# Two attention layers in fp32: groups 2 and 3 of layer 1 split as well, sums seeded by plain DMAs, and four smaller shifts in order

## The chip, the cores and the metric

The kernel runs on one core of one Trainium2 chip. The metric is the device time of one execution in microseconds. Before the change three runs took 3254.99, 3256.44 and 3256.32 us, median 3256.32. A change within about 0.2% is not told from none.

## What is computed

The input x is 4 x 128 x 64 x 64 in fp32: four images b of C = 128 channels and N = 4096 positions. Two attention layers follow each other.

```
layer 0 (inner width 64):
  g, theta, phi = g_w x + g_b, theta_w x + theta_b, phi_w x + phi_b
  y = softmax(theta^T phi) g          # over 4096 keys
  x1 = W_w y + W_b + x
layer 1 (width 128):
  q, k, v = Wq x1 + bq, (sum over o of Wk) * x1 + bk, Wv x1 + bv
  out = x1 + softmax(q^T k / sqrt(128)) v
```

The phi and k biases and the q bias are scaled by 64, so the scores are large, and the softmax needs an exact maximum shift and products of nearly full fp32 precision.

## The kernel before

**Stages and blocks.** A stage is one layer of one image, and there are eight: layer 0 of images 0 and 1, then layer 1 of 0, layer 0 of 2, layer 1 of 1, layer 0 of 3, layer 1 of 2, layer 1 of 3 (`run_all`). A stage has 8 blocks of 512 queries, numbered g over the whole program, 64 in all. A block walks over the 4096 keys in 16 groups `s`; a group is two key tiles of 128, and its scores are 128 keys x 1024 (two tiles x 512 queries) in PSUM, double buffered as `scores[:, s % 2]`. While one stage runs, its blocks also prepare the keys and values of a later one: phi and g (`prepares="phi"`), k and v (`"kv"`), or k and v with v held aside in `hold` and `g_vals` (`"late"`, the stage before the last). The last stage prepares nothing.

**Each engine has its own written order.** `block_program` of an engine goes through s = 0 to 15 and issues what falls due at that group; constants such as `G_AT`, `MOVES_AT`, `PIECES_AT` say at which. Engines meet only at semaphores. An instruction that waits holds all that comes behind it on its engine.

**Rough pieces.** The softmax shift is the row maximum of rough scores. For the next block's 512 queries, 32 matmuls (`rough_piece`, L510), four query tiles by eight key chunks, go into two PSUM banks of `rough` in turn, and DVE reduces each (`reduce_piece`, L924). `PIECES_AT` gives two pieces to most groups and three to four of them (in layer 1 s = 7, 8, 10, 12). In layer 1 a group with three issues one piece ahead of its scores and two behind. DVE then builds a diagonal (L931), PE turns it into a row (`shift_row`, L516) at s = 15.

**Layer 0.** Scores of a tile are two fp32r matmuls (L534, L537). ACT takes the exponential straight from PSUM (L841). POOL adds the 16 groups up in `sums` (L385, `add`). The values are full fp32 matmuls, two column halves at a time (L573, `value_batch`).

**Layer 1.** Scores of a tile are three fp32r matmuls (L539, L540, L543), high by high, high key low part by query, key by low query part. DVE adds the shift row from PSUM into one of six SBUF buffers `probs` (L941). ACT takes the exponential twice: rounded to fp32r into one of four `p_hi` buffers (L834), and in place (L835, semaphore `s_whole`). POOL subtracts the two into `p_lo` (`split_probs`, L1046, `s_p_lo`). PE multiplies three groups behind the scores (`LAG` = 3): per tile `p_hi v_hi`, `p_lo v_hi`, `p_hi v_lo` (`halved_values`, L559 to L561). So the value matmuls of group 13, 14 and 15 run at s = 0, 1, 2 of the next block. Groups 2 and 3, `WHOLE`, are the exception: no `p_hi`, no split, but true fp32 matmuls with `v_vals` (`value_group`, L582), each recorded as two instructions, so four a group.

**The sums of layer 1.** For the denominators the 16 exponentials are summed in two tiles `sent_sums[:, 0]` and `[:, 1]`. POOL first seeds them with additions of groups 0 + 1 and 2 + 3 (`seed`, L1078), then for each of groups 4 to 15, right behind its split, POOL issues a DMA that adds the group into tile s % 2 (`send`, L1089, `accum_op=add`, 512 KB). A send waits until the one two groups before has landed. In the next block at s = 2 POOL folds both tiles into `total` (`fold`, L367, L371); PE makes denominators (L607) at s = 5.

**Low part of the queries.** ACT copies the projected queries twice, plain (`q_whole`) and rounded (`qry_a`); POOL subtracts into `qry_b` at s = 9 (`split_q`).

**Late values.** In the last block of the stage before the last, and in the first of the last, ACT moves held v chunks into `v_hi`, and POOL subtracts into `v_lo` (`split_held`), at the groups in `MOVES_AT`.

**SP's queue** in a block: load x_kv, load x_q, then wait for the previous block's result, store it, load the residual.

Of the kernel before, what the change touches and what calls it, by code (L numbers as in the profile page):

```python
# [51 lines left out]
WHOLE_CHUNK = 1  # L52
WHOLE = (2, 3)
HALVED = tuple(s for s in range(16) if s not in WHOLE)
SEEDS = 2
SEED_AT = {2: 0, 3: 2}
SENT = tuple(range(4, 16))
# [46 lines left out]
def build(nc, x, consts, out):  # L104
# [16 lines left out]
    with ExitStack() as ctx:  # L121
# [21 lines left out]
        v_vals = sb("v_vals", [P, QB])  # L143
        v_hi = sb("v_hi", [P, BLOCKS - 1, QB], F32R)
        v_lo = sb("v_lo", [P, BLOCKS - 1, QB], F32R)
# [6 lines left out]
        q_whole = sb("q_whole", [P, QB])  # L152
# [7 lines left out]
        diag = sb("diag", [P, 2, QB], F32R)  # L160
        piece_max = sb("piece_max", [P, SUB, BLOCKS])
        sums = sb("sums", [P, GC])
        sent_sums = sb("sent_sums", [P, TPG, GC])
# [4 lines left out]
        rdiag = sb("rdiag", [P, 2, QB], F32R)  # L168
        result = sb("result", [P, QB])
# [51 lines left out]
        s_seed = sem("s_seed")  # L221
        s_sent = [sem(f"s_sent_{n}") for n in range(TPG)]
# [75 lines left out]
        def seeded(nth, s):  # L298

            return nth * SEEDS + s // 2 + 1  # L300

        def sent(nth, s):

            return 16 * (nth * len(SENT) // TPG + (s - SENT[0]) // TPG + 1)

        def v_lows(b, c):

            return b * (BLOCKS - 1) + v_chunk(c) + 1

        def v_chunk(c):  # L310

            return c - (c > WHOLE_CHUNK)
# [4 lines left out]

        def summed(eng, nth, s):

            if s < 2 * SEEDS:  # L320
                eng.wait_ge(s_seed, seeded(nth, s))
            else:
                eng.wait_ge(s_sent[s % TPG], sent(nth, s))
# [15 lines left out]
        def probs_free_1(eng, st, s):  # L339

            if s >= SHARP_BUFS or st.prev == 1:
                nth, g, last = st.nth, st.g, s - SHARP_BUFS
                if last < 0:
                    nth, g, last = st.prev_nth, st.g - 1, last + GROUPS
                if last in WHOLE:
                    eng.wait_ge(s_used, used(g, last))
                else:
                    eng.wait_ge(s_p_lo, halved(nth, last))
# [10 lines left out]
        def fold(eng, layer, g, nth):  # L359
# [13 lines left out]
        def add(eng, st, s):  # L373
# [5 lines left out]
            if s == 1:  # L379
                if st.prev == 0:  # L380
                    eng.wait_ge(s_fold, st.g)
# [5 lines left out]
        def halved(nth, s):  # L387

            return nth * len(HALVED) + HALVED.index(s) + 1
# [784 lines left out]
```

## Time and profile before

| | |
|---|---|
| median of three runs | 3256.32 us |
| the profiled execution | 3254.69 us |
| its span, first to last instruction | 3252.9 us |
| PE busy | 3204.8 us (99%) |
| POOL busy | 3020.9 us (93%) |
| DVE, ACT busy | 2088.1 us (64%), 1897.1 us (58%) |
| granted TensorE clock | 0.998 |

The busy time of an engine is the union of its instructions' spans. Matmuls overlap in the records, since their ends are modelled: the distance from one start to the next is PE's pace, not the length of a record. A block is read here from one shift-row matmul (L516) to the next.

### The profile page before, as it was taken

To read this page: it belongs to the slowest core of one execution; us is meant where nothing else is said; L and a number is where in the kernel's file an instruction comes from. 1 tells how busy PE (TensorE), PEld (TensorE's weight loads), DVE (VectorE), ACT (ScalarE), POOL (GpSimd) and SP (SyncE) were. 2 spreads that over 40 slices of the span, in tenths; PEclk is the share of its full clock that TensorE was granted. 3 is DMA by queue.
4 is the path that set the end of the run, shared out by engine and by line. 5 is a ranking of instruction groups with operands and counts; after the bars stand their busy time and mean duration, and the time that the engine had idled before them with its cause. 6 is when DMAs were issued, how large, how long until landed. Compare 5 with 4: busy or idle time off the path is not lost. (4 is left out here: it accounts for less than half of the span.)

```text
span 3252.9 us, 38831 instructions
## 1 busy us (share of the span) xinstructions
PE 3204.8 (99%) x13636; PEld 2199.8 (68%) x13636; DVE 2088.1 (64%) x3036; ACT 1897.1 (58%) x2473; POOL 3020.9 (93%) x1611
## 2 busy tenths in 40 slices
PE   8999999999999999999999999999999999999997
PEld 5555555557777775555777776555577777777775
DVE  5555555556777765555777776555577777777773
ACT  5555455556666665455666665555566666666665
POOL 6988999998999999999999999999899999999998
PEclk9999999999999999999999999999999999999999
DMA  1000000004665640000565664000066675657566
GB/s 52 26 20 26 23 27 26 27 23 94 136 136 119 143 101 27 26 27 27 107 142 114 141 131 101 22 22 26 27 136 136 125 144 115 128 117 143 117 136 120
DMA packets 91922, 271.45 MB, mean 83 GB/s; under 512 B 10192, under 2 KB 10192, under 8 KB 91728
## 3 DMA queue, kind: packets, MB, share of 16 engines
q0 software_dynamic: 55296, 201.35, 32.2%
q1 hardware_dynamic: 36432, 67.62, 6.8%
q8 instruction: 108, 1.77, 0.2%
q14 instruction: 86, 0.70, 0.1%
HBM read 50.83 MB, written 16.78 MB: 21 GB/s over the span
## 5 line engine op out<-in xcount | busy, mean ns | idle before, releaser
L924 DVE TENSOR_REDUCE piece_max<-rough 128x1 f32<-128x512 f32 x2032 | 1314.7, 683 | 657.1 <-PE rough L510 646.9
L1046 POOL TENSOR_TENSOR p_lo<-probs,p_hi 128x1024 fp32r<-128x1024 f32 x448 | 1191.4, 2712 | 64.4 <-ACT probs L835 54.0
L385 POOL TENSOR_TENSOR sums<-sums,probs 128x1024 f32<-128x1024 f32 x448 | 1067.1, 2382 | 110.4 <-ACT probs L841 70.3
L941 DVE TENSOR_TENSOR probs<-scores,shift_rows 128x1024 f32<-128x1024 f32 x512 | 626.2, 1223 | 470.1 <-PE scores L543 466.9
L841 ACT ACTIVATE probs<-scores 128x1024 f32<-128x1024 f32 x512 | 521.0, 1024 | 654.3 <-PE scores L537 653.5
L834 ACT ACTIVATE p_hi<-probs 128x1024 fp32r<-128x1024 f32 x448 | 474.5, 1059 | 558.6 <-DVE probs L941 558.4
L510 PE MATMUL rough<-keys_a,qry_a 128*128 128x512 f32 x2032 | 714.2, 420 | 11.3 <-POOL keys_a L1046 3.2
L835 ACT ACTIVATE probs<-probs 128x1024 f32<-128x1024 f32 x512 | 535.7, 1046 | 88.8 <-DVE probs L941 88.8
L510 PEld LDWEIGHTS rough<-keys_a,qry_a 128*128 128x128 f32 x2032 | 366.4, 188 | 276.5 <-DVE piece_max L924 151.9
L1089 POOL DMA_DIRECT2D sent_sums<-probs x384 | 442.3, 1152 | 0.2 <-issue 0.2
L539 PE MATMUL scores<-qry_a,keys_a 128*128 128x512 f32 x1024 | 425.7, 416 | 0.0
L534 PE MATMUL scores<-qry_a,keys_a 128*128 128x512 f32 x1024 | 423.3, 413 | 0.0
L537 PE MATMUL scores<-qry_b,keys_b 128*128 128x512 f32 x1024 | 403.2, 394 | 0.0
L543 PE MATMUL scores<-qry_b,keys_a 128*128 128x512 f32 x1024 | 399.8, 390 | 0.0
L540 PE MATMUL scores<-qry_a,keys_b 128*128 128x512 f32 x1024 | 399.8, 390 | 0.0
L573 PE MATMUL acc_out<-probs,g_vals 128*64 128x512 f32 x1536 | 371.9, 605 | 0.0
L559 PE MATMUL acc_out<-p_hi,v_hi 128*128 128x512 f32 x896 | 351.9, 393 | 8.7 <-POOL p_lo L1046 8.7
L561 PE MATMUL acc_out<-p_hi,v_lo 128*128 128x512 f32 x896 | 349.2, 390 | 0.0
L560 PE MATMUL acc_out<-p_lo,v_hi 128*128 128x512 f32 x896 | 348.8, 389 | 0.0
L534 PEld LDWEIGHTS scores<-qry_a,keys_a 128*128 128x128 f32 x1024 | 192.6, 188 | 98.2 <-issue 36.5
L539 PEld LDWEIGHTS scores<-qry_a,keys_a 128*128 128x128 f32 x1024 | 192.7, 188 | 57.4 <-issue 17.3
L540 PEld LDWEIGHTS scores<-qry_a,keys_b 128*128 128x128 f32 x1024 | 192.4, 188 | 53.9 <-issue 15.1
(94 smaller groups left out, 3172.6 us busy)
## 6 DMA issues: line engine op xcount, KB each, us to landing
sent_sums<-probs POOLq DMA_DIRECT2D x384, 512.0 KB, 4.9
x_q<-x SPq DMA_DIRECT2D x32, 256.0 KB, 2.7
x_res<-x SPq DMA_DIRECT2D x32, 256.0 KB, 2.9
mid<-mid_new SPq DMA_DIRECT2D x32, 256.0 KB, 2.2
x_kv<-mid SPq DMA_DIRECT2D x32, 256.0 KB, 2.7
x_q<-mid SPq DMA_DIRECT2D x32, 256.0 KB, 2.7
x_res<-mid SPq DMA_DIRECT2D x32, 256.0 KB, 4.5
out<-result SPq DMA_DIRECT2D x32, 256.0 KB, 3.4
```

The costliest lines, as they stand in the source:

```text
L385: eng.tensor_tensor(sums[:], sums[:], probs[:, slot(st, s)], ALU.add).then_inc(s_plus, 1)
L510: mm(place, qry_a[:, parity, t * P:(t + 1) * P], cols(keys, c), start=True, stop=True).then_inc(s_rough, 1)
L534: mm(place, hi[:, k], qa, start=True, stop=False)
L539: mm(place, hi[:, k], qa, start=True, stop=False)
L540: mm(place, lo[:, k], qa, start=False, stop=False)
L834: nc.scalar.activation(hi_part(s), place, ACT.Exp, scale=SCALES[1])
L835: nc.scalar.activation(place, place, ACT.Exp, scale=SCALES[1]).then_inc(s_whole, 1)
L841: nc.scalar.activation(probs[:, slot(st, s)], scores[:, s % 2], ACT.Exp, scale=SCALES[0]).then_inc(s_whole, 1)
L924: nc.vector.reduce_max(piece_max[:, t, c:c + 1], src, AX.X).then_inc(s_reduced, 1)
L941: nc.vector.tensor_tensor(probs[:, slot(st, s)].rearrange("p (h c) -> p h c", c=QB), scores[:, s % 2].rearrange("p (h c) -> p h c", c=QB), ...
L1046: nc.gpsimd.tensor_tensor(dst, w, rd(hi), ALU.subtract).then_inc(done, 1)
L1089: nc.gpsimd.dma_start(sent_sums[:, s % TPG], probs[:, slot(st, s)], accum_op=ALU.add).then_inc(s_sent[s % TPG], 16)
```

## The change

- `WHOLE` is gone. All 16 groups of layer 1 are split: each gets `p_hi`, a split on POOL and six fp32r value matmuls. `v_vals` and `value_group` go; `v_hi` and `v_lo` have all eight chunks.
- The seeds go. SP copies groups 0 and 1 into the two sum tiles with plain DMAs (`copy_probs`), POOL sends groups 2 to 15. The sum tiles exist twice, by parity of the block. For groups 14 and 15 the send stands ahead of the split, for the others behind.
- `q_whole` goes. ACT makes `qry_a` alone, ahead of group 15's exponential in both layers (in layer 0 it stood behind). DVE makes `qry_b` from PSUM at the end of its block. The second rough piece of a block waits for that.
- In layer 1 the first of three rough pieces goes between the two score tiles of its group.
- `G_AT` for blocks that follow a layer 1 block goes from 11 to 12. The held values are moved at other groups, three in the one block and five in the next; before it was five (one without a split) and three.
- `diag` and `sums` now lie in other tiles' memory.

```diff
-PHI_AT, G_AT = (11, 9), (13, 11)
+PHI_AT, G_AT = (11, 9), (13, 12)
-MOVES_AT = ({6: 0, 8: 1, 10: 2, 12: 3, 14: 4}, {1: 5, 3: 6, 5: 7})
+MOVES_AT = ({6: 0, 9: 1, 12: 2}, {5: 3, 7: 4, 9: 5, 11: 6, 13: 7})
-Q_LO_AT = 9
-WHOLE_CHUNK = 1
-WHOLE = (2, 3)
-SEED_AT = {2: 0, 3: 2}
-SENT = tuple(range(4, 16))
+COPIED = (0, 1)
...
+        def summed(eng, nth, s):
+            if s in COPIED:
+                eng.wait_ge(s_copied[s], 16 * nth + 16)
+            else:
+                eng.wait_ge(sent_sem(nth, s), sent(nth, s))
...
+            def copy_probs(st, s):                                   # SP
+                sp.wait_ge(s_whole, whole_of(st.g, s))
+                if s == COPIED[0]:
+                    sp.wait_ge(s_fold, st.g - (st.prev == 1))
+                settle(sp)
+                sp.dma_start(sent_sums[:, st.parity, s], probs[:, slot(st, s)]).then_inc(s_copied[s], 16)
...
                 if st.next_q:
                     load_q(st.g + 2, *st.next_q)
+                if st.layer == 1:
+                    for s in COPIED:
+                        copy_probs(st, s)
...
                     place = scores[:, s % 2, h * QB:(h + 1) * QB]    # PE, score_group
+                    if h == 1 and between is not None:
+                        between()
...
+                    if m == 1:                                       # PE, piece
+                        pe.wait_ge(l_q, st.g + 2)
...
-                    if st.layer == 1 and st.nxt is not None and at[s] == 3:
-                        piece()
-                    score_group(st, s)
+                    score_group(st, s, piece if st.layer == 1 and st.nxt is not None and at[s] == 3 else None)
...
-                    if s == GROUPS - 1 and st.next_q:                # ACT
-                        take_q_whole(st.g + 2, st.next_q[0], two_banks(1))
...
+                    if s == GROUPS - 1 and st.next_q:
+                        act.wait_ge(s_scores, (st.g + 1) * GROUPS)
+                        take_q_hi(st.g + 2, st.next_q[0], st.parity, two_banks(1))
                     if st.layer == 0:
                         probs_direct(st, s)
-                    if s == GROUPS - 1 and st.next_q:
-                        act.wait_ge(s_scores, (st.g + 1) * GROUPS)
-                        take_q_hi(st.next_q[0], st.parity, two_banks(1))
...
+            def split_q(g, layer, parity, src):                      # DVE
+                dve.wait_ge(h_q, g + 1)
+                nc.vector.scalar_tensor_tensor(out=qry_b[:, parity], in0=src, scalar=(TH_B, Q_B)[layer],
+                                               in1=rd(qry_a[:, parity]), op0=ALU.add,
+                                               op1=ALU.subtract).then_inc(l_q, 1)
...
             def send(st, s):                                         # POOL
                 pool.wait_ge(s_whole, whole_of(st.g, s))
+                summed(pool, st.nth, s - TPG)
                 settle(pool)
+                nc.gpsimd.dma_start(sent_sums[:, st.parity, s % TPG], probs[:, slot(st, s)],
+                                    accum_op=ALU.add).then_inc(sent_sem(st.nth, s), 16)
...
-                    if st.layer == 1 and s in HALVED:
+                    if st.layer == 1 and s >= GROUPS - TPG:
+                        send(st, s)
+                    if st.layer == 1:
                         split_probs(st, s)
-                    if st.layer == 1 and s in SENT:
+                    if st.layer == 1 and s not in COPIED and s < GROUPS - TPG:
                         send(st, s)
-                    if st.layer == 1 and s in SEED_AT:
-                        seed(st, SEED_AT[s])
-                    if s == Q_LO_AT and st.nxt is not None:
-                        split_q(st.g + 1, 1 - st.parity)
```

## Rows read from the trace of the kernel before

**Rows 1.** The page, its first part: busy time and instructions of each engine.

```profile
PE 3204.8 (99%) x13636; PEld 2199.8 (68%) x13636; DVE 2088.1 (64%) x3036; ACT 1897.1 (58%) x2473; POOL 3020.9 (93%) x1611
```

**Rows 2.** Sums by stretch, one block each.

```profile
core 0: us, PE busy (x) PEld busy (x) DVE busy (x) ACT busy (x) POOL busy (x), PEclk, DMA share, GB/s
1363.35:1406.45 43.10, 43.10 (x184) 24.53 (x183) 23.66 (x40) 22.30 (x32) 39.38 (x19) 1.00 0.09 25
962.78:1019.67 56.89, 56.46 (x245) 44.18 (x243) 41.54 (x55) 36.67 (x47) 54.60 (x33) 1.00 0.63 130
2562.41:2618.28 55.87, 55.58 (x243) 43.81 (x241) 41.53 (x55) 36.48 (x46) 54.65 (x33) 1.00 0.65 132
2785.89:2845.42 59.53, 56.50 (x235) 42.24 (x233) 41.63 (x55) 37.19 (x47) 59.31 (x37) 1.00 0.59 116
3011.54:3066.90 55.36, 54.97 (x235) 42.83 (x233) 41.53 (x55) 34.59 (x43) 53.50 (x32) 1.00 0.64 129
```

**Rows 3.** Timeline of PE, a phi block: start us, us, engine, line, tiles, shape, count.

```profile
982.87 1.96 PE L582 MATMUL acc_out<-probs,v_vals 128*128 128x512 f32 x4
...
984.91 0.39 PE L540 MATMUL scores<-qry_a,keys_b 128*128 128x512 f32 x1
...
986.50 1.88 PE L582 MATMUL acc_out<-probs,v_vals 128*128 128x512 f32 x4
...
988.68 0.40 PE L540 MATMUL scores<-qry_a,keys_b 128*128 128x512 f32 x1
...
990.53 0.39 PE L560 MATMUL acc_out<-p_lo,v_hi 128*128 128x512 f32 x1
...
991.44 0.39 PE L561 MATMUL acc_out<-p_hi,v_lo 128*128 128x512 f32 x1
991.92 0.50 PE L510 MATMUL rough<-keys_a,qry_a 128*128 128x512 f32 x1
992.25 0.40 PE L539 MATMUL scores<-qry_a,keys_a 128*128 128x512 f32 x1
```

**Rows 4.** Timeline of PE, the same block at group 11.

```profile
1006.36 0.39 PE L561 MATMUL acc_out<-p_hi,v_lo 128*128 128x512 f32 x1
1007.09 1.10 PE L499 MATMUL acc_out<-const_sb,x_kv 128*128 128x64 f32 x8 [0.34 <-ACT keys_a L756]
```

**Rows 5.** Timeline of DVE, the block of rows 3.

```profile
991.18 1.96 DVE L924 TENSOR_REDUCE piece_max<-rough 128x1 f32<-128x512 f32 x3
```

**Rows 6.** Timeline of ACT, the end of a layer 0 block.

```profile
1278.98 0.67 ACT L756 ACTIVATE qry_a<-rough,const_sb 128x512 fp32r<-128x512 f32 x1
```

**Rows 7.** Timeline of PE, the start of the layer 0 block after.

```profile
1280.83 0.40 PE L534 MATMUL scores<-qry_a,keys_a 128*128 128x512 f32 x1
```

**Rows 8.** Timeline of POOL, the block of rows 3.

```profile
974.81 2.41 POOL L367 TENSOR_TENSOR sent_sums<-sent_sums 128x1024 f32<-128x1024 f32 x1
...
978.73 4.74 POOL L1078 TENSOR_TENSOR sent_sums<-probs 128x1024 f32<-128x1024 f32 x2
983.43 2.38 POOL L1046 TENSOR_TENSOR p_lo<-probs,p_hi 128x1024 fp32r<-128x1024 f32 x1
985.76 0.87 POOL L1089 DMA_DIRECT2D sent_sums<-probs  x1
986.37 2.66 POOL L1046 TENSOR_TENSOR p_lo<-probs,p_hi 128x1024 fp32r<-128x1024 f32 x1
```

**Rows 9.** Line 1046, subtractions of held values: ns min/median/max.

```profile
L1046 POOL TENSOR_TENSOR v_lo<-hold,v_hi x4: 1264/2778/3732, 2794.4 to 2819.7; 128x512 fp32r<-128x512 f32 x4
```

**Rows 10.** Line 1089, the accumulating DMAs: issue to landing.

```profile
DMA to landing us min/median/max: 4.4/4.9/7.7
```

**Rows 11.** Timeline of POOL, the last block.

```profile
3209.15 1.75 POOL L1089 DMA_DIRECT2D sent_sums<-probs  x1
...
3212.75 1.44 POOL L1089 DMA_DIRECT2D sent_sums<-probs  x1
...
3234.75 2.25 POOL L1089 DMA_DIRECT2D sent_sums<-probs  x1
```

More of the change, by code:

```diff
@@ L357, in shifted, with fold @@
             return nth * GROUPS + s + 1
-        def fold(eng, layer, g, nth):
+        def fold(eng, layer, g, nth, parity):
             if layer == 0:
@@ L701, in block_program @@
                         if stage.prepares == "kv":
[L702 to L704 removed]
+                            pe.wait_ge(l_v, stage.made * BLOCKS + st.i + 1)
                         if stage.opening and st.i_known < BLOCKS - 1:
@@ L759, in scaled, with take_q_hi @@
                 return nc.scalar.activation(dst, src, ACT.Copy, scale=scale)
-            def take_q_whole(g, layer, src):
+            def take_q_hi(g, layer, parity, src):
                 act.wait_ge(p_q, g + 1)
-                if not (isinstance(g, int) and g == 0):
-                    act.wait_ge(l_q, g)
-                copy(q_whole[:], src, (TH_B, Q_B)[layer])
-            def take_q_hi(layer, parity, src):
                 copy(qry_a[:, parity], src, (TH_B, Q_B)[layer]).then_inc(h_q, 1)
@@ L799, in move_v @@
                 act.wait_ge(h_hold, c + 1)
-                copy(v_vals[:] if c == WHOLE_CHUNK else v_hi[:, v_chunk(c)], held(c)).then_inc(h_v, 1)
+                copy(v_hi[:, c], held(c)).then_inc(h_v, 1)
             def shift_to_row(layer, g, parity):
@@ L999, in _ @@
             dve.wait_ge(s_vec, 2)
+            split_q(0, 0, 0, rough[:, 0:QB])
             for m, piece in enumerate(pieces):
                 reduce_piece(m, piece, four_banks[m % SUB])
-            shift(0, 0)
+            shift(0)
+            split_q(1, 0, 1, rough[:, 0:QB])
             def block_program(st):
@@ L1031, in block_program @@
                         m += 1
-                    if s == V_LO_AT and st.stage.prepares == "kv" and st.i != WHOLE_CHUNK:
+                    if s == V_LO_AT and st.stage.prepares == "kv":
                         split_v(st.stage.made * BLOCKS + st.i, st.i, acc_out[:, 1 - st.parity])
+                if st.next_q:
+                    split_q(st.g + 2, st.next_q[0], st.parity, two_banks(1))
                 if st.ends:
-                    fold(dve, st.layer, st.g, st.nth)
+                    fold(dve, st.layer, st.g, st.nth, st.parity)
                     reciprocals(st.g, st.parity)
@@ L1125, in block_program @@
                         c = MOVES_AT[0][s - 1]
-                        if c != WHOLE_CHUNK:
-                            split_held(stage.made * BLOCKS + c, c)
+                        split_held(stage.made * BLOCKS + c, c)
             run_all(pool, block_program)
```

141 lines of the change are left out of this document (46 added, 95 removed).

## The prediction, made before any run of the change

> **What bounds the kernel now.** First the page's busy times: PE 3204.8 us, 99% of the span [rows 1]. Then the sums by stretch, one block each, cut at the shift-row matmul [rows 2]. A layer 0 block takes 43.10 us with PE never idle and POOL busy 39.38. A layer 1 block takes 56.89 us where phi and g are prepared, 55.87 where k and v are held for later, 55.36 where nothing is prepared; PE is busy all but 0.3 to 0.4 us of it and POOL 53.5 to 54.7, so two engines are in question. I call these phi, late and plain blocks. There are 14 phi blocks that follow a layer 1 block, 2 that follow layer 0, 8 late ones, 8 in the last stage.
>
> Busy PE is not PE at its pace, so the third view is PE's timeline, read by distances between starts. From L560 at 990.53 to L561 at 991.44 are four fp32r matmuls: 0.2275 us each [rows 3]. Four fp32 records of a whole group have starts (1.88-0.59)/3 = 0.43 apart. Small matmuls (x8 in 1.10, the last of about 0.28) stand 0.117 apart [rows 4]. A plain block has 96 score, 32 rough, 84 value and 3 row matmuls in fp32r, 215 x 0.2275 = 48.9; 8 whole-value and 2 query records, 4.3; 8 denominators, 0.9: 54.1 us. It takes 55.36, so 1.25 us are stalls that the busy time hides. A late block has eight more small ones (0.9): 55.0 against 55.87, 0.85 of stalls. A phi block has two more fp32 records and eight small ones (1.8): 55.9 against 56.89, 1.0. PE's count of instructions sets every L1 block, with about 1 us of stalls on top.
>
> **Groups 2 and 3 are split too.** Removed: per block two whole groups. From the first record at 982.87 to the second score matmul at 984.91 are 2.04 us, from 986.50 to 988.68 are 2.18 [rows 3]. Put in: six fp32r matmuls each, 1.365, then the same followers: one more pitch in the first case (1.59), two in the second (1.82). Gain 0.45 + 0.36 = 0.81 us a block, 25.9 us over 32, all on PE.
>
> The Trainium skill ("FP8 and Floating Point Precision", TensorE Precision Notes) says that a true fp32 matmul makes four passes through the array. By that and the pitch of rows 3 four tiles would save one pass each, 0.91 a block and 29.1 in all; the trace's 0.86 for a tile is 3.8 passes, close to it, and the sum stays with the rows.
>
> **The third rough piece.** The piece ahead of the scores waits for a reduction: L561 at 991.44, L510 at 991.92, then 0.33 instead of 0.23 to L539 [rows 3]. That is 0.25 + 0.11 = 0.36 late. It recurs, less or more, at the groups with three pieces, where no fp32 work ahead covers it. In its new place it comes 0.68 later and that wait is gone. What is late next: the third piece of the group needs the bank of this one. From its start, its own 0.39 and some 0.03 of signal, a reduction of 0.683, and about 0.16 until PE runs again (the reduction of 991.18 ends at 991.86, and L539 one pitch later than the piece puts that effectively at 992.02) [rows 3, 5] make 1.26. The third comes at 0.2275 x (1+3+1) = 1.14. So 0.12 stays, four times a block, 0.48. The bounds are 0 and 0.36 each; I take 0.12. Net: plain 1.25 to 0.48, late 0.85 to 0.48, phi 0.5 to 0.48.
>
> **g at 12 instead of 11.** In phi blocks the g projection waits for ACT: L561 at 1006.36, L499 at 1007.09, 0.50 over its pitch [rows 4]. One group later (over 3 us) the keys are there, and ACT's copy of g still lies ahead of the row at 15. 14 x 0.5 = 7 us. The blocks after layer 0 keep 13.
>
> **q without q_whole.** ACT drops a 0.67 us copy, POOL a subtraction, DVE gets one. In layer 0 ACT now does it before group 15's exponential. Its start was 1278.98 [rows 6]; it moves up to about 1278.1, the exponential back by 0.67 to about 1279.8, and PE needs that one only with group 1 of the next block, at 1280.83 [rows 7]. DVE's q low is ready about 1.4 us after the copy starts, 1279.5, before the second piece, one pitch ahead of that score. In layer 1 the copy stays in place and DVE has idle time. Cost 0. Nothing can be won, since PE does not wait for q now; if the cover were gone, each us of delay would cost up to 64 us in all.
>
> **POOL and the sends.** Removed per L1 block: two seeds, 4.70 (978.73 to 983.43), and the q subtraction, 1.26. Added: two splits at 2.33 (983.43 to 985.76) and two sends at 0.61 (to the next start), 5.88 [rows 8, 9]. Fold 3.92 (974.81 to 978.73). POOL's round is 16 x 2.33 + 14 x 0.61 + 3.92 = 49.7, with k or phi 51.0, as before (51.1). But each send waits for the landing of the one two before it. At POOL's own pace they are 5.9 apart; landing takes 4.4 to 7.7 us, median 4.9 [rows 10]. DMA share rises from 0.63 [rows 2] by 14/12 and two SP copies, to about 0.8. Where out store and residual load run beside the sends I expect 1.4 us of waiting. Groups 14 and 15 now send before they split: when POOL is behind ACT, send 14 comes 0.61 after send 13, and send 12 is 3 us old, so about 2.1 + 0.3 more is lost. Bounds for the waits are 0 and 7; I take 3.8. The round is then 53.5 plain, 54.8 late and phi. PE's new rounds: plain 53.8, late 54.7, phi 55.6. So POOL stays just inside in phi and plain, and is level in late.
>
> Does PE wait for p_lo of group 2 after the fold, which the whole groups hid? The fold ends 15.8 us into the block, split 2 at 18.2, PE wants it at 20.1 (982.87-962.78) [rows 3]. Slack 1.9, then growing, since PE takes 3.2 a group or more and POOL 2.94. Gone if the fold slips by 2. SP's copies of groups 0 and 1 stand ahead of the out store and the residual load, which wait until group 9 anyway. Copy 1 can start when split 1 can, at 974.81-2.33 = 972.5; with the median landing of rows 10 it is there at 977.4, with the longest at 980.2, and send 2 comes at 981.0. Cost 0.
>
> **Late low parts.** Three moves in the last late block, five in the next, each 1.26 [rows 9]. Before, the 59.53 us block had POOL busy 59.31 [rows 2]. Now POOL needs 50 + 5 x 1.26 + waits, about 58.5, and the block before 57.5: both are POOL's. With the one after, 170 instead of 170.9. Between this and PE's pace (165) I take -3. The last block is POOL's and the landings': sends at 3209.15 to 3234.75 stand 3.20 apart on the mean [rows 11]. Two groups more at 3.1 against seeds: +1.5; the last send no longer follows the last split: -1. I take +0.5.
>
> **Sum,** on the profiled execution's own 3254.69 us (span 3252.9 and 1.8 around it; 1.6 below the median of the runs): phi 14 x (0.81+0.5) = -18.3; two phi after layer 0 and one late after it, -3.2; late 6 x 0.8 = -4.8 (held back by POOL); plain 5 x 1.45 = -7.2; moves -3; last +0.5; layer 0, 32 blocks, 0. Together -36.0: 3218.7, against the median 3220. I forecast 3219.
>
> **Rivals.** (B) PE alone decides: the sends do not hold POOL and the last third-piece stall is under something. Then 0.12 x 4 x 29 = 14 less, 3205. For it: POOL's work is unchanged in sum. Against: landing takes longer than 5.9 in part of the sends. The Trainium skill ("DMA: Bandwidth & Descriptors", Anatomy of one DMA) gives 2.0 us plus bytes over 436e3 for such a DMA, an estimate of 3.2 us for 512 KB, which would leave no wait and lead to this case; the shortest landing here is 4.4 [rows 10], so the trace is against it.
> (C) The waits are 5 us and more. A round of 56.2 gives phi -0.7, late +0.3, plain -0.4, moves +1, the rest -2: -11, 3245. For it: POOL has no reserve left in late blocks.
> (D) Slower: the landings pace the round. With p from send to send it is 14p + 9.85; it passes 56.89 at p = 3.36. POOL's own pace is 2.94, the last block has 3.20 and once 3.60 [rows 11]. At 3.5: 58.85, 2 x 14 + 3 x 6 + 2.2 x 8 = +64, 3320. Against: in the last block POOL is always behind, and elsewhere fold, k and phi give the queue rest.
> (E) Nothing moves, because the stalls return in other places: 3256. Against: 25.9 us are PE's instruction time.
>
> **Chances.** Forecast 0.50, B 0.25, C 0.13, D 0.08, E 0.04. A measurement here tells 0.2% (6.5 us) from no change. Faster 0.86, within 0.06, slower 0.08. Range 3200 to 3246: B with its bound, and most of C; the forecast's own is 3210 to 3230.
>
> **What would show it.** Right: phi blocks near 55.6, late 54.8, plain 53.9, layer 0 at 43.1; no L582 line; L499 right behind L561; DMA landings 5 to 6. Wrong: PE idle before the split value matmuls with POOL as releaser (C or D), a second rough piece waiting for the DVE's q low, layer 0 blocks off 43.1, or POOL busy over 55 in phi blocks.

## The result and the profile after

The change makes the kernel slower: 3287.97 us median of 4 runs (3285.12 to 3290.38) against 3255.99 beside it, a ratio of 1.0099 [1.0086, 1.0111]. The forecast was 3219, range 3200 to 3246. The profiled execution has a span of 3285.0 us, 32.1 more than before.

First the page's busy times, as [rows 1]:

```profile
PE 3210.3 (98%) x13764; PEld 2222.6 (68%) x13764; DVE 2140.9 (65%) x3103; ACT 1924.1 (59%) x2473; POOL 3010.0 (92%) x1612
```

Then sums by stretch with the columns of [rows 2]: layer 0; an early phi block (18), a later one (38), the last of its stage (39); a late block; block 56, where held values are moved; a plain one.

```profile
1409.39:1452.49 43.10, 43.10 (x184) 24.54 (x183) 24.43 (x41) 21.73 (x30) 38.24 (x18) 1.00 0.09 25
847.11:903.18 56.07, 56.07 (x249) 44.84 (x248) 42.37 (x56) 38.14 (x47) 54.46 (x35) 1.00 0.78 166
1885.72:1944.00 58.28, 56.54 (x248) 44.68 (x247) 42.37 (x56) 38.13 (x47) 55.46 (x34) 1.00 0.77 163
1944.00:2007.28 63.28, 58.30 (x248) 46.09 (x247) 42.47 (x56) 38.11 (x47) 58.26 (x35) 0.97 0.74 158
2577.93:2634.84 56.91, 55.88 (x247) 44.31 (x246) 42.37 (x56) 37.91 (x46) 55.74 (x35) 1.00 0.79 167
2805.98:2866.59 60.61, 56.37 (x239) 42.95 (x237) 42.46 (x56) 38.52 (x48) 60.53 (x40) 1.00 0.72 153
3037.01:3093.46 56.45, 54.76 (x238) 43.42 (x237) 42.37 (x56) 36.03 (x43) 55.02 (x34) 1.00 0.77 164
```

Layer 0 hasn't moved. Early phi blocks run as forecast in kind (56.07 for 56.89). Then the rounds grow (a round is what POOL does from one block's start to the next) until PE idles 1.7 us in one and 5.0 in the last of the stage, with POOL busy 55 us and more: above the 55 that the prediction named as the sign of its being wrong. Block 39 has a second loss: behind PE's wait of 3.31 us that ends at 1994.67, the granted clock is at 1.2 GHz from 1995.9 to 1999.3 and fp32r matmuls start 0.43 us apart in place of 0.23, which makes the 0.97 in its row. Before the change no stretch of the kernel, its first 45 and last 13 us aside, ran at that level; now three do, 10.2 us together. What PE waits for stands in the page's costliest groups:

```profile
L553 PE MATMUL acc_out<-p_hi,v_hi 128*128 128x512 f32 x1024 | 414.4, 405 | 43.8 <-POOL p_lo L1026 43.1
```

Before, the same line had 8.7 us of such idle time. PE's timeline in block 39, as [rows 3], shows one of these waits, and POOL's shows its cause:

```profile
1952.27 0.50 PE L553 MATMUL acc_out<-p_hi,v_hi 128*128 128x512 f32 x1 [1.51 <-POOL p_lo L1026]
```

```profile
1941.92 1.84 POOL L1050 DMA_DIRECT2D sent_sums<-probs  x1
1942.53 3.67 POOL L1026 TENSOR_TENSOR p_lo<-probs,p_hi 128x1024 fp32r<-128x1024 f32 x1
1944.88 2.16 POOL L1050 DMA_DIRECT2D sent_sums<-probs  x1
1948.94 0.86 POOL L1050 DMA_DIRECT2D sent_sums<-probs  x1 [1.91 <-issue]
1949.51 2.71 POOL L1026 TENSOR_TENSOR p_lo<-probs,p_hi 128x1024 fp32r<-128x1024 f32 x1
1951.84 1.21 POOL L1050 DMA_DIRECT2D sent_sums<-probs  x1
```

The send of group 14 starts at 1948.94, when that of group 12 (issued at 1941.92) has landed, and the split of group 14 stands behind it. Its split ends at 1949.51 + 2.71 = 1952.22, and PE goes on at 1952.27. The instruction's end releases PE, not its start plus 2.33: these lines are to be read by their ends. That reading was missing from the prediction.

Blocks by kind, us, each from shift row to shift row, with the forecast's terms taken from before:

| blocks | before | forecast | after |
|---|---|---|---|
| 12 phi (17-22, 33-38) | 682.7 | 667 | 688.8 |
| 23 and 39 | 114.7 | 112 | 123.9 |
| 16, 32, 48 | 174.0 | 171 | 171.4 |
| late, 49 to 54 | 335.1 | 330 | 338.8 |
| 55 to 57, held values | 170.9 | 168 | 177.3 |
| plain, 58 to 62 | 275.9 | 269 | 279.0 |
| 63, the last | 76.2 | 76.7 | 80.6 |
| all else | 1423.5 | 1423.5 | 1425.4 |

### The profile page after: what moved, and what is told of

It reads as the page before. It is cut to its first block and busy times, and to the rows that moved or that the text cites. A ratio compares the mean times of both kernels' runs of the same rounds, so it can differ in the third digit from the quotient of the medians.

```text
span 3285.0 us, 39340 instructions
## 1 busy us (share of the span) xinstructions
PE 3210.3 (98%) x13764; PEld 2222.6 (68%) x13764; DVE 2140.9 (65%) x3103; ACT 1924.1 (59%) x2473; POOL 3010.0 (92%) x1612
## 5 line engine op out<-in xcount | busy, mean ns | idle before, releaser
L1026 POOL TENSOR_TENSOR p_lo<-probs,p_hi 128x1024 fp32r<-128x1024 f32 x512 | 1498.5, 3143 | 19.7 <-ACT probs L809 17.5
L367 POOL TENSOR_TENSOR sent_sums<-sent_sums,probs 128x1024 f32<-128x1024 f32 x448 | 1068.2, 2384 | 146.9 <-ACT probs L815 104.1
L808 ACT ACTIVATE p_hi<-probs 128x1024 fp32r<-128x1024 f32 x512 | 542.9, 1060 | 617.0 <-DVE probs L911 616.9
L1050 POOL DMA_DIRECT2D sent_sums<-probs x448 | 670.6, 1498 | 56.7 <-issue 34.9
L553 PE MATMUL acc_out<-p_hi,v_hi 128*128 128x512 f32 x1024 | 414.4, 405 | 43.8 <-POOL p_lo L1026 43.1
L555 PE MATMUL acc_out<-p_hi,v_lo 128*128 128x512 f32 x1024 | 402.5, 393 | 0.0
L554 PE MATMUL acc_out<-p_lo,v_hi 128*128 128x512 f32 x1024 | 401.9, 392 | 0.0
L553 PEld LDWEIGHTS acc_out<-p_hi,v_hi 128*128 128x128 f32 x1024 | 192.7, 188 | 109.4 <-POOL p_lo L1026 71.2
L528 PEld LDWEIGHTS scores<-qry_a,keys_a 128*128 128x128 f32 x1024 | 192.7, 188 | 98.0 <-issue 59.2
```

The source lines that it names most:

```text
L367: eng.tensor_tensor(sums, sums, probs[:, slot(st, s)], ALU.add).then_inc(s_plus, 1)
L528: mm(place, hi[:, k], qa, start=True, stop=False)
L553: mm(acc_out[:, parity], hi, hi_part(s)[:, at], start=tile == 0, stop=False)
L808: nc.scalar.activation(hi_part(s), place, ACT.Exp, scale=SCALES[1])
L1026: nc.gpsimd.tensor_tensor(dst, w, rd(hi), ALU.subtract).then_inc(done, 1)
L1050: nc.gpsimd.dma_start(sent_sums[:, st.parity, s % TPG], probs[:, slot(st, s)], accum_op=ALU.add).then_inc(sent_sem(st.nth, s), 16)
```

## The experiments

The recorded expectations call the exponentials of a group s a list, and some call PE TensorE and DVE VectorE. Three theories stood at the start. T1: POOL waits for landings, above all where a send stands ahead of a split. T2: POOL has too many instructions. T3: the new order on PE and DVE costs. Each result is the median with its ratio to the kernel before, run beside it.

**Order of sends 14 and 15** (on the changed kernel)

```diff
-                    if st.layer == 1 and s >= GROUPS - TPG:
-                        send(st, s)
...
-                    if st.layer == 1 and s not in COPIED and s < GROUPS - TPG:
+                    if st.layer == 1 and s not in COPIED:      # behind split_probs
```

> The changed kernel with one thing undone: sends 14 and 15 stand behind their splits like the others. Theory T1 (POOL waits for landings, most of all because a send that waits stands ahead of a split): the stalls of PE before value groups 13 to 15 at the start of a block shrink, phi blocks go from 57.1 to 58.6 back to under 57, time 3240 to 3262. Theory T2 (POOL has too many instructions, the place of the waits is no matter): within 0.3% of 3288. Theory T3 (the new order on PE and DVE costs it): 3288.

Measured 3262.3, ratio 1.002 [1.001, 1.0029]. 26 us come back, at the upper end of T1's range and far from T2's and T3's. The 12 phi blocks fall to 674.8, but 23 and 39 stay at 59.6 and 64.1. Most phi blocks now take 55.9 to 56.1, but 37 takes 59.2. POOL's and PE's timelines and sums by stretch show why:

```profile
1829.53 2.40 POOL L349 TENSOR_TENSOR sent_sums<-sent_sums 128x1024 f32<-128x1024 f32 x1 [1.14 <-DMA sent_sums<-probs]
```

```profile
1835.68 0.50 PE L553 MATMUL acc_out<-p_hi,v_hi 128*128 128x512 f32 x1 [1.20 <-POOL p_lo L1026]
```

```profile
1837.11:1840.53 3.42, 3.42 (x9) 2.65 (x9) 0.52 (x1) 0.00 (x0) 3.42 (x3) 0.50 0.80 156
```

The fold (L349) waits 1.14 us for a landing, PE then idles 1.20 for a split behind it, and behind that the granted clock is at half for 3.4 us.

**Short sends**

```diff
-dma_start(sent_sums[:, st.parity, s % TPG], probs[:, slot(st, s)], ...
+dma_start(sent_sums[:, st.parity, s % TPG, 0:QB // 2], probs[:, slot(st, s), 0:QB // 2], ...
```

> The changed kernel with all sends cut to the first 256 of 1024 columns, so the sums miss the rest; every instruction, wait and semaphore stays, only the bytes of the accumulating DMAs fall to a quarter. T1: landings fall to about 3 us, POOL no longer waits, all phi blocks run at the 56.1 of the first ones, late 55.0, plain 55.2 at most: 3225 to 3238. T2: the issue of a send costs POOL the same, so 3280 or more. T3: 3288.

Measured 3238.7, 0.9949 [0.9933, 0.9966]: 49 us back, 1 us beyond T1's range and against T2 and T3. The sums lack three quarters of what the 14 sends add, so this is a kernel for timing only. Blocks 23 and 39 fall to 57.9 and 57.8; 55 to 57 fall to 174.1, as in the run before.

**Fold on DVE**

```diff
+                    if st.prev == 1 and s == FOLD_AT[1][0]:     # DVE
+                        fold(dve, *before(st))
...
-                    if s == FOLD_AT[st.prev][st.layer]:         # POOL
+                    if st.prev == 0 and s == FOLD_AT[0][st.layer]:
```

> The changed kernel with the fold of layer 1's sums (2.4 and 1.3 us on POOL, with gaps 3.9) moved to DVE at group 3, where DVE has idle time. POOL has 3.9 us less in each round, the sends start earlier in the block and stand further apart over the round. T2: POOL's round falls under PE's, 3230 to 3245. T1: as much or nearly, since earlier sends take the pressure off the landings, but the waits at groups 14 and 15 (up to 3 us a block) stay: 3235 to 3265. T3: 3288.

Measured 3385.7, 1.04 [1.0384, 1.0415], though it takes POOL's fold away. DVE's second add of the fold has two SBUF inputs, and the line's min/median/max is

```profile
L353 DVE TENSOR_TENSOR total<-sent_sums x32: 691/2766/2774, 808.1 to 3372.3; 128x512 f32<-128x512 f32 x32
```

In 26 of the 32 cases a tensor operation of POOL is running when it starts, and it ends some 0.55 us after that one, having taken 2.75 us or more; in the six others it takes 0.69. DVE's shifts and piece reductions come late behind it, and PE waits 75.6 us for reductions. The Trainium skill ("SBUF — State Buffer", SBUF: two separate sides) says that a DVE operation with two SBUF inputs and a GpSimd operation that reads SBUF lock each other out of a shared port pair, for the whole of the one that started first; the trace agrees, by those 0.55 us. The granted clock is at 1.2 GHz for 164 us of this run in all. So it moved the load to a worse place and tells nothing of POOL.

**The order on PE alone** (on the kernel before)

```diff
-PHI_AT, G_AT = (11, 9), (13, 11)
+PHI_AT, G_AT = (11, 9), (13, 12)
...
+                    score_group(st, s, piece if ... at[s] == 3 else None)
```

> The kernel before with two parts of the change alone: the third rough piece between the score tiles, and g projected at group 12. Groups 2 and 3 stay whole, POOL as before. If these do what the prediction said: phi -0.5, late -0.4, plain -0.8 us a block, 3241 to 3248. If the third-piece stall only moves (its new stalls in the changed kernel add up to about 0.65 a block): 3247 to 3253, most of it g's. T3: slower than 3256.

Measured 3249.0, 0.998 [0.9971, 0.9989]. Plain blocks 54.8 for 55.36, late 55.68, phi 56.59. T3 falls for PE's new order; DVE's part of it, the queries' low part, comes below.

**Third piece back, ahead of the scores** (on the kernel with sends behind)

```diff
-score_group(st, s, piece if ... at[s] == 3 else None)
+if ... at[s] == 3:
+    piece()
+score_group(st, s)
```

> The changed kernel with sends behind their splits (e1, 3262) and, beside it, the third rough piece ahead of the scores again. From e4 and the records (stall 0.36 and more before, four of 0.16 after) the move should be worth 0.5 in plain blocks, 0.2 in late ones, nothing or a small loss in phi blocks: so 3 to 8 us slower than e1, 3265 to 3271, if PE sets the blocks. If POOL and the landings set them, taking the PE gain away changes less than 3 us: 3259 to 3265. If the move was part of the loss: under 3259.

Measured 3263.5, 1.0026 [1.0015, 1.0036]. PE's pace worsens (phi 56.37, late 55.56, plain 55.04, where the piece between the tiles gives 55.94, 55.0 and, in the fastest block, 54.1), yet the total moves by 1 us: with sends of full size most of what PE wins by the new place is lost again in waits for POOL. In phi blocks it wins 0.43, where nothing was expected.

**Seeds on POOL again**, both in place of the SP copies (12 sends), and one of them (13 sends)

```diff
-                sp.dma_start(sent_sums[:, st.parity, s], probs[:, slot(st, s)])
...
+                nc.gpsimd.tensor_tensor(sent_sums[:, st.parity, s // 2], probs[:, slot(st, s)],
+                                        probs[:, slot(st, s + 1)], ALU.add)
```

> e1 with the seeds back on POOL: two additions of 2.4 us, twelve sends instead of fourteen, no copies by SP. POOL has 3.5 us more of instructions in a round (53 to 54.5 of about 55.5), the DMA engines four transfers of 512 KB less. T1 (the landings of sends are what holds POOL): landings back to 4.9, the odd blocks of 58 to 60 us go, 3235 to 3258. T2 (POOL's instruction count): rounds of 55 to 56.5 everywhere, 3255 to 3285.

> Between e1 and e6: one seed on POOL (groups 0 + 1), one copy by SP (group 2), thirteen sends. POOL has 1.8 us more of instructions than e1, the DMA engines two transfers less. T1: between, better than e1, 3240 to 3260. T2: slower than e1 (3262). If both matter about as much, this is the best of the three.

Measured 3326.2 (1.0218 [1.0203, 1.0233]) and 3291.1 (1.0105 [1.0088, 1.0121]). Fewer bytes and more instructions make it slower, against both of T1's ranges, so T1 alone can't hold. The first is beyond T2's range (3255 to 3285) too.

**Queries' low part on DVE too** (on the run with the order alone; groups 2 and 3 stay whole)

```diff
-                copy(q_whole[:], src, (TH_B, Q_B)[layer])
...
+                nc.vector.scalar_tensor_tensor(out=qry_b[:, parity], in0=src, scalar=(TH_B, Q_B)[layer], ...
```

> Groups 2 and 3 whole again: e4 (the kernel before with the third piece between the tiles and g at 12; 3249) and beside it the query part of the change: no q_whole, low part on DVE. POOL has 1.26 us less in every block. If the query part costs nothing, as predicted: 3243 to 3250, the small gain in the last phi blocks of a stage (58.3 in e4) and the blocks of the moved values, where POOL is behind. If the wait for DVE's low part at the second piece costs PE anything: over 3250.

Measured 3244.9, 0.9967 [0.9955, 0.9979]: with two groups whole, both edits together are a gain of 11 us, and DVE's part costs nothing that shows. That ends T3.

**Both edits of the first two runs at once**

> The changed kernel with both edits at once: sends of lists 14 and 15 behind their splits (order, 3288.0 to 3262.3 alone), and all 16 sends cut to 256 of their 1,024 columns (bytes, 3288.0 to 3238.7 alone). The sums of the other columns miss a part. If order and bytes act through one thing, the wait of POOL for the landing of lists 12 and 13 ahead of splits 14 and 15, then with short landings the order is worth next to nothing: 3234 to 3239. If the two are separate losses, they add: near 3213. T2 (instructions of POOL's round) keeps what is left above 3219 in the blocks with moved values and at the end: blocks 55 to 57 stay near 174 us together, 63 near 76.

Measured 3237.2, 0.9944 [0.993, 0.9957], like short sends alone (14 sends, not the 16 of the expectation). Order and bytes act through one thing, the landing. But 18 us above the forecast remain where next to nothing (1 us in all) is waited for a landing. Two blocks of this run and POOL's timeline in it:

```profile
1015.56:1071.46 55.90, 55.90 (x249) 44.85 (x247) 42.34 (x56) 38.12 (x47) 55.53 (x34) 1.00 0.33 72
3050.39:3104.73 54.34, 54.34 (x239) 43.57 (x237) 42.36 (x56) 36.03 (x43) 54.26 (x34) 1.00 0.32 68
```

```profile
2959.62 2.40 POOL L1026 TENSOR_TENSOR p_lo<-probs,p_hi 128x1024 fp32r<-128x1024 f32 x1
2961.96 0.87 POOL L1050 DMA_DIRECT2D sent_sums<-probs  x1
2962.57 2.69 POOL L1026 TENSOR_TENSOR p_lo<-probs,p_hi 128x1024 fp32r<-128x1024 f32 x1
2964.92 1.17 POOL L1050 DMA_DIRECT2D sent_sums<-probs  x1
2965.53 3.00 POOL L1026 TENSOR_TENSOR p_lo<-probs,p_hi 128x1024 fp32r<-128x1024 f32 x1
...
2986.27 5.17 POOL L1026 TENSOR_TENSOR p_lo<-probs,p_hi 128x1024 fp32r<-128x1024 f32 x1
2988.62 3.65 POOL L1050 DMA_DIRECT2D sent_sums<-probs  x1
2989.52 5.18 POOL L1026 TENSOR_TENSOR p_lo<-probs,p_hi 128x1024 fp32r<-128x1024 f32 x1
2991.88 3.67 POOL L1050 DMA_DIRECT2D sent_sums<-probs  x1
```

The starts of the splits stand 2.96 apart, their ends 3.24 to 3.27: 2962.02, 2965.26, 2968.53. The records' lengths grow (2.40, 2.69, 3.00, up to 5.18) because the starts run ahead of the work. Once they are 5.2 long the starts, too, stand 3.25 and more apart. By the ends a split behind a send takes 2.44 and a send 0.84; a split behind a split takes 2.36, so a send costs POOL 0.92 with what it adds to the split behind it. [Rows 8] had it: the ends there are 985.81, 986.63, 989.03, so 0.82 and 2.40, where the prediction read 2.33 and 0.61.

This gives a new T2': POOL's round goes by ends. 14 x 2.44 + 2 x 2.36 + 14 x 0.84 + fold 3.7 = 54.3 in a plain block, with phi's or k's 1.24 it is 55.6. The two rows show POOL busy 54.26 and 55.53.

**Moved values as before** (on sends behind)

```diff
-MOVES_AT = ({6: 0, 9: 1, 12: 2}, {5: 3, 7: 4, 9: 5, 11: 6, 13: 7})
+MOVES_AT = ({6: 0, 8: 1, 10: 2, 12: 3, 14: 4}, {1: 5, 3: 6, 5: 7})
```

> The changed kernel with sends 14 and 15 behind their splits (3262.3), and the moved values placed as before: five in block 55 (at 6, 8, 10, 12, 14), three in block 56, none in 57. Blocks 55 to 57 together are 170.9 us before the change, 174.1 with the spread. If the spread is what costs there: their sum falls to about 171, the total to about 3259. If POOL's longer round with 16 splits is what costs and the place of the moved values doesn't matter: sum at 174 or more, total 3262 or more.

Measured 3261.8, 1.0019 [1.001, 1.0028]; blocks 55 to 57 together 176.2. The place of the values isn't the cause. Its POOL timeline shows where a landing is waited for once the sends stand behind:

```profile
2965.32 1.47 POOL L1050 DMA_DIRECT2D sent_sums<-probs  x1
2965.93 5.67 POOL L1026 TENSOR_TENSOR p_lo<-probs,p_hi 128x1024 fp32r<-128x1024 f32 x2
2973.59 2.40 POOL L349 TENSOR_TENSOR sent_sums<-sent_sums 128x1024 f32<-128x1024 f32 x1 [1.99 <-DMA sent_sums<-probs]
```

The fold waits for send 15, which runs beside the SP copies of the next groups 0 and 1 and lands 8.1 us after its issue.

**phi blocks with the old order** (on the kernel of 3244.9, which has 12 sends)

```diff
+                    if three and stage.prepares == "phi":
+                        piece()
...
```

> Eight groups of before's 14 sends and two whole groups kept, third piece between score tiles and g at 12, queries' low part on VectorE (3244.9), but in the 16 blocks that prepare phi the third piece stays ahead of the scores. There it cost +0.2 us a block between the tiles. If that is a cost of its place: 14 blocks x 0.2 = 3 us less, and blocks 23 and 39 fall from 58.0 towards 57.4: 3240 to 3242. If it came from g's new place, or POOL sets the pace there: 3245 or more.

Measured 3245.8, 0.997 [0.9959, 0.9982]; phi blocks 56.67 against 56.60. No gain: both places cost the same there.

**One whole group, seeds on POOL** (on the run before)

```diff
-WHOLE = (2, 3)
+WHOLE = (3,)
```

> As the kernel with phi's order of before, but group 2 split too, with one whole group left (3). Seeds still added by POOL, no SP copies. POOL gets one more split, about +2.3 us a round; TensorE loses half the gain that two more split groups give, 0.33 us a block x 32 = 11 us at best. If POOL bears it: 3230 to 3235. If POOL's round has no reserve from there on, as the 16 split groups say: 3245 to 3280, with POOL above 55.5 us busy in phi's blocks and TensorE waiting on p_lo.

Measured 3261.7, 1.0019 [1.001, 1.0028]. One more split of 2.4 us costs 16 us in all, with 12 sends and bytes as before. phi blocks are at 56.37, TensorE's pace; 39 is at 61.6, block 56 at 63.4, block 63 at 80.8.

**Sends in pairs**

```diff
-                nc.gpsimd.dma_start(sent_sums[:, st.parity, s % TPG], probs[:, slot(st, s)], ...
+                nc.gpsimd.dma_start(sent_sums[:, st.parity], probs[:, first:first + TPG], ...
```

> The changed kernel with its sends joined in pairs: lists s and s+1 go with one send into both sum tiles, behind the odd list's split, 7 sends a block in place of 14; bytes as before; lists 14 and 15 behind their splits too. The ends of POOL's instructions in the trace stand 3.27 us apart for a split and a send (2.43 + 0.84) where the starts stand 2.96 apart: a send takes 0.84 to 0.9 of POOL, not the 0.61 of the prediction, and this hardly depends on bytes (0.84 with 256 columns too). If that is the term that failed (T2': POOL's round is 16 x 2.4 + 14 x 0.87 + 3.7 = 54.3 before any wait), seven sends less give POOL 6 us a block back: phi blocks 55.9, late 55.0, plain 54.0, no step at 23 and 39 above 58, last block 77 to 79; total 3222 to 3232. If landings decide (T1): 1 MB a send lands some 6 us after its end, each pair waits for the one before, the fold waits for the last: blocks over 57, total above 3262. If a send's cost on POOL goes by bytes after all: near 3262.

Measured 3487.3, 1.0707 [1.0691, 1.0723]: the way that T1 gave (blocks over 57, above 3262, with no upper end), against T2', and far more than was expected. A pair's send takes 0.88, about as one group's does, but it lands 6.0 us after its end at the least, and the next pair waits for it while the splits stand behind:

```profile
1712.57 5.07 POOL L1025 TENSOR_TENSOR p_lo<-probs,p_hi 128x1024 fp32r<-128x1024 f32 x2
1719.57 0.88 POOL L1051 DMA_DIRECT2D sent_sums<-probs  x1 [1.92 <-DMA sent_sums<-probs]
1720.17 2.70 POOL L1025 TENSOR_TENSOR p_lo<-probs,p_hi 128x1024 fp32r<-128x1024 f32 x1
```

Pairs stand 7.6 apart (1711.96 to 1719.57), beyond PE's 6.8 to 7: phi blocks take 63. The granted clock is at 1.2 GHz for 164 us of the run, behind PE's waits; how much of the 7% that makes isn't parted from the waits themselves.

**Half the sends left out** (on both edits at once)

```diff
-                    if st.layer == 1 and s not in COPIED:
+                    if st.layer == 1 and s not in COPIED and s % TPG == 0:
```

> The changed kernel with sends 14 and 15 behind their splits, sends cut to 256 columns (3237.2 so far) and the seven sends of odd lists left out altogether: the sums miss these lists and the other columns. No landing is waited for in either; only the number of sends on POOL differs, 14 to 7. T2': 7 x 0.87 = 6.1 us less of POOL's round, which is on the path in plain blocks (54.3 with POOL busy all through), in blocks 55 to 57 (174.2) and at the end: plain 54.0, sum of 55 to 57 about 168, 3222 to 3230. If the sends' instructions cost nothing beside the landings: 3237 as before.

Measured 3211.7, 0.9865 [0.9849, 0.9882]: 25.5 us under the run with both edits at once, in which splits and sends waited 1 us in all for landings: this is the count of sends, and more than T2' asked for. The sums lack more still, so this too is for timing only. The answering blocks:

```profile
1015.56:1071.49 55.93, 55.93 (x248) 44.85 (x247) 42.37 (x56) 38.13 (x47) 49.11 (x26) 1.00 0.22 55
3036.67:3090.77 54.10, 54.10 (x239) 43.57 (x237) 42.37 (x56) 36.03 (x43) 47.85 (x25) 1.00 0.21 51
```

POOL is busy 6.4 us less a round, 7 x 0.92. Blocks 55 to 57 fall from 174.2 to 163.3, the last from 78.4 to 66.4; phi blocks don't move.

**One whole group, SP copies and 14 sends** (on sends behind), and the same with the moved values as before

```diff
+WHOLE = (3,)
+HALVED = tuple(s for s in range(16) if s not in WHOLE)
-                    if st.layer == 1:                    # POOL
+                    if st.layer == 1 and s in HALVED:
                         split_probs(st, s)
```

> The changed kernel with sends 14 and 15 behind their splits (3262.3) and group 3 alone whole again (its values as two fp32 matmuls, no split, no high part): SP copies, 14 sends, all else as changed, and the output tiles of the two layers share memory to make room. By ends POOL's round falls by one split, 2.4 us: 15 x 2.4 + 14 x 0.87 + 3.7 = 51.9 plain, 53.2 with phi or k. TensorE pays half of what the two split groups gave, some 0.35 a block. If POOL's round in instructions is what the change lacks (T2'): phi 56.3, late 55.3, plain 54.4, sum of 55 to 57 near 170, 3232 to 3242, the best so far. If the landings decide by themselves (T1), as in e1 with 14 sends: blocks that jump by 2 to 4 us remain, 3250 to 3262.

> The kernel before this one in the call, with the moved values at the places of the kernel before (five, then three). With 16 splits the place didn't matter (3261.8 against 3262.3), since POOL was behind in all these blocks. With one split less POOL has about 2 us of reserve a block: the spread should then serve better, this one 1 to 3 us slower; equal within 1 us if it doesn't matter here either.

Measured 3240.4 (3239.65 to 3242.86), 0.9953 [0.994, 0.9965], the fastest with whole sums, 15 to 16 us under before; and 3241.9, 0.9954 [0.9941, 0.9968]. Blocks 55 to 57 take 173.1 and 172.7: the spread doesn't matter here either.

```profile
1017.24:1073.50 56.26, 56.26 (x246) 44.48 (x245) 42.37 (x56) 37.18 (x46) 53.02 (x33) 1.00 0.79 169
3056.41:3110.89 54.48, 54.48 (x237) 43.20 (x235) 42.38 (x56) 35.07 (x42) 51.74 (x31) 1.00 0.79 169
```

All 14 full sends and the 0.79 of DMA share are there, and PE is not idle in these blocks. By ends POOL's sends wait 38.4 us in all for landings in this run, 34.6 of it at group 4 in 29 rounds, and PE doesn't feel it there. The landings do harm only where POOL has no reserve.

The runs in one table. POOL's round in a phi block is summed from 2.44 for a split behind a send, 2.36 for others and for a seed, 0.84 for a send, 3.7 for the fold, 1.24 for phi:

| kernel | round by ends | phi block, median | total |
|---|---|---|---|
| half the sends (short) | 49.1 | 55.93 | 3211.7 |
| one whole, copies, 14 sends | 53.1 | 56.27 | 3240.4 |
| two whole, q low on DVE | 53.7 | 56.60 | 3244.9 |
| all split, short sends behind | 55.6 | 55.93 | 3237.2 |
| all split, sends behind | 55.6 | 55.94 | 3262.3 |
| one whole, POOL seeds | 56.1 | 56.37 | 3261.7 |
| one seed, 13 sends | 57.0 | 56.93 | 3291.1 |
| two seeds, 12 sends | 58.5 | 58.22 | 3326.2 |

Where the round passes PE's 55.9 to 56.4, in the last two rows, the median block is as long as POOL's round, though single blocks differ (56.8 to 61.7 in the last row). Below that, most phi blocks go at PE's pace and the totals differ by waits elsewhere, above all in blocks 23, 39, 55 to 57 and 63.

**The clock's part.** Between full and short sends, both behind their splits, the profiled spans differ by 26.0 us (3262.5 and 3236.5). The pages have PE busy 3203.7 and 3192.2, so 14.5 of it is longer idle time and 11.5 longer work. The second is the granted clock: it is at 1.2 GHz in seven stretches, 27.3 us in all, of the one kernel and in none of the other, the start and end of both aside. At 0.43 us for 0.23 that is up to 13 us. By the ends of POOL's instructions the first kernel waits 12.7 us for landings at the fold, in 16 of its rounds, and 12.3 at sends, of which 10.9 stand at group 9 and next to nothing at 14 and 15. That is a count in one trace and not an experiment, but it says that the fold and the single sends share the loss about evenly.

## Why the prediction was wrong

**The step "POOL and the sends" failed, in two of its terms.** The first is the send: "two sends at 0.61 (to the next start)". By ends it is 0.84, and a split behind one 2.44, so a group costs 3.27 and not 2.94. Over 14 sends this is 4.6 us: the round is 54.3 plain and 55.6 with k or phi, not 49.7 and 51.0. The warning stood in [rows 2]: POOL was busy 54.60 where the prediction summed 51.1 for the same block of before, and the 3.2 apart of [rows 11] was put down to landings. The second is the waits. The prediction put 3.8 us of them on a round too short by 4.6 and came out just under PE's pace, so it priced them at nothing on PE outside the late blocks. By ends (what a send's end stands later than 0.84 after the end before it) the sends of the changed kernel wait 57.5 us in all for landings, 1.8 a round and half of the 3.8: 36.4 of it at group 14, in 28 of 32 rounds, 14.5 at group 15, 4.8 at group 9. 55.6 + 1.8 = 57.4 is what the 12 phi blocks take on the mean. The true round leaves 0.3 us under PE's 55.9 in phi, and is above it in late (55.6 to 55.0) and plain blocks (54.3 to 54.1); with short sends the late blocks climb from 54.97 to 55.59 as POOL falls behind. So waits for a landing are lost, and not made good later. Of the 69 us between the forecast and 3288.0, 51 go with the landings (3288.0 to 3237.2) and 18 remain without them.

What the waits are is settled by the four runs of order and bytes: 3288.0, 3262.3 (order), 3238.7 (bytes), 3237.2 (both). A full send lands 3.6 us after its own end in most rounds for groups 2 to 6, and over 5 in a tenth of all cases, up to 7.0; other transfers lengthen it. Send 15 shows that: at the median it lands 3.63 after its end before the change and in the run with both seeds on POOL, where SP copies nothing, but 4.92 in the changed kernel and 4.79 with the sends behind their splits, where the copies of the next groups 0 and 1 run beside it. The prediction had the copies at cost 0. With the sends behind their splits the fold is due two splits, 4.8 us, behind the end of send 15, so a landing at 3.63 wouldn't hold it; the 12.7 us that it waits there go with the copies, by the trace, and no run leaves the copies out by themselves. Send 14 ahead of its split comes 0.84 after send 13 in place of 3.27 and waits for send 12; the prediction saw this wait (2.1 + 0.3) but booked it on POOL alone, though the split of the same group, and PE, stand behind it. Rival C (3245) had the mechanism, a POOL without reserve, but took the waits too long (5 and more) and the round too short (56.2); rival D (3320) had the sign, but its pacing by landings is shown only in the run with pairs.

**"Late low parts"** was put at -3 and came out at +6.4. It rests on the same round: 5 x 1.26 on top of 54.3 is 60.6, measured 60.61 in block 56. The spread itself is worth nothing in the total (two runs, on 16 and on 15 splits). **The last block**, +0.5 forecast, is +4.4, for the same reason: with seven sends fewer it loses 12 us. **Blocks 23 and 39** had no term of their own. There POOL's phi part comes at the end of a block in which POOL is behind, and PE waits for it ahead of the first rough pieces on the new keys:

```profile
1994.67 0.73 PE L502 MATMUL rough<-keys_a,qry_a 128*128 128x512 f32 x2 [3.31 <-POOL keys_a L1026]
```

They grow by 9.2 us together: 7.5 is longer idle time of PE, and the rest about what the stretch at 1.2 GHz in block 39 costs.

**PE's steps held, a little under size.** A split group after an L588, and g behind its values, in block 18, as [rows 3, 4]:

```profile
867.29 0.50 PE L553 MATMUL acc_out<-p_hi,v_hi 128*128 128x512 f32 x1
...
868.98 0.39 PE L534 MATMUL scores<-qry_a,keys_b 128*128 128x512 f32 x1
```

```profile
892.09 0.76 PE L502 MATMUL rough<-keys_a,qry_a 128*128 128x512 f32 x2
892.69 0.40 PE L553 MATMUL acc_out<-p_hi,v_hi 128*128 128x512 f32 x1
...
893.85 0.40 PE L555 MATMUL acc_out<-p_hi,v_lo 128*128 128x512 f32 x1
894.08 1.00 PE L491 MATMUL acc_out<-const_sb,x_kv 128*128 128x64 f32 x8
```

Group 2 takes 1.69 to the second score matmul where 1.59 was forecast and 2.04 stood before. The two groups give 0.66 (56.59 in the run with the order alone, 55.93 with all split), not 0.81. g's wait is gone at its place, L491 starts 0.23 after L555, but the block gains only 0.20 of the 0.5 (56.87 before, 56.67 in the run with phi's old order, where g alone of PE's work has moved): the term was too large. Two pieces from 892.09 should end at 892.55 and PE goes on at 892.69: 0.14 to 0.16 stays of the third piece's stall, against 0.12. In phi blocks moving the piece brought 0.07 (56.67 to 56.60) with two whole groups, but 0.43 (56.37 to 55.94) with all split, where 0.02 was forecast. In the other order of steps, then, splitting brings only 0.30 (56.67 to 56.37), and the two terms can't be priced apart: together 0.73 in place of 0.83. With short sends and half of them left out, phi, late and plain blocks take 55.93, 54.97 and 54.10; forecast were PE rounds of 55.6, 54.7 and 53.8. Had POOL been free, this kernel would have come near the forecast, and a little below (3211.7, with the last block shortened as well). The forecast's sum puts 1.45 on a plain block where its own terms give 1.58, worth 0.6 us in all. **q** cost nothing: layer 0 blocks stand at 43.10.

Not settled: how much of the 26 us of the order is the clock's, and how long PE would have waited in blocks 23 and 39 had POOL's phi part come earlier; no run parts these.

## What to carry to other kernels

Sum GpSimd's round from the distances between the ends of its instructions, and hold the sum against its busy time in the same block: if the busy time is larger, a cost is misread, and reserve that seems to be there isn't. When a second engine is about level with the one that sets the pace (here 55.6 us of 55.9), a saving on the first is bought with every wait of the second, so give it back a piece of work before adding one: here the sends behind their splits took the loss from 1.0% to 0.2%, and one whole group kept, which costs TensorE 0.35 us a block, turned that into a gain of 0.5%. Look at the granted clock behind each wait of TensorE: a wait of 1.2 us cost block 37 3.3. A DMA that must wait for an earlier one belongs behind the work that others wait for, and its landing is to be counted from its end.

## What the runs showed of the hardware

- Sending costs GpSimd by the instruction, not by bytes: 0.84 us at 128 KB, 0.84 at 512 KB, 0.88 at 1 MB.
- GpSimd's records start ahead of the work: in a run of splits and sends each record is 0.3 us longer than the one before, up to about 5.2. The climb of issue-to-landing times from 4.5 to 5.8 us (medians of groups 2 to 6 in the changed kernel) is that lead; from the send's end they stay at 3.6.
- From the end of the send, the shortest landings of an accumulating SBUF to SBUF transfer are 1.71 us for 128 KB, 3.57 for 512 KB and 6.00 for 1 MB: 211 to 216 GB/s between them. With the send's own 0.84 added, and less bytes over that rate, the 128 KB take 1.94 us. The Trainium skill ("DMA: Bandwidth & Descriptors", Anatomy of one DMA) has 2.0 us fixed plus bytes over 436e3; the trace agrees with the fixed part, and shows half of the rate.
- A DVE add of 512 columns with two SBUF inputs takes 2.77 us in place of 0.69 when a tensor operation of GpSimd is running as it starts, and ends 0.55 us after that one.
- The granted TensorE clock falls to 1.2 GHz behind some waits of PE and not behind others: behind 3.31 us at 1994.67 and 2.16 at 2876.23 in the changed kernel, not behind 1.56 at 1835.43; with the sends behind their splits, behind 1.20 at 1835.68.
